# Experts of a perceiver block on one core: up products with the weights stationary and the row columns moving

## The chip, the cores and the metric

The kernel runs on one core of one Trainium2 chip, as a single program: a cross attention, a self attention and a feed-forward part with a shared expert and eight routed ones. The metric is the device time of one execution in microseconds. TensorE multiplies: it loads a stationary operand of up to 128 x 128 (LDWEIGHTS, "PEld" in the profile) and streams a moving operand through it (MATMUL, "PE"), with the result in PSUM. ScalarE (ACT), VectorE (DVE) and GpSimd (POOL) do the elementwise work.

## The reference

Only the last part of the reference matters here. `x` is (8, 128, 512), so 1024 tokens of width 512; the hidden width is 1024.

```python
def _L0_ffn_ref(x, Wg, Wu, Wd, W1, W2):
    xt = x.reshape(T, D)
    probs = jax.nn.softmax(xt @ Wg, axis=-1)
    topv, topi = jax.lax.top_k(probs, 2)
    topv = topv / jnp.sum(topv, axis=-1, keepdims=True)
    cw = jnp.zeros((T, E), x.dtype).at[jnp.arange(T)[:, None], topi].set(topv)
    h = _gelu(jnp.einsum('td,edf->tef', xt, Wu))
    y = jnp.einsum('tef,efd->ted', h, Wd)
    moe = jnp.einsum('ted,te->td', y, cw)
    shared = _gelu(xt @ W1) @ W2
    return (shared + moe).reshape(B, S, D)
x = x + _L0_ffn_ref(_layernorm(x), ...)
```

## The kernel before

The experts' part is the function `experts`. Tokens are handled as tiles of 128 rows: 8 tiles (`NT`) for the shared expert, whose rows are the tokens in order, then the tiles of the eight routed experts, into which each token's normalised row was scattered twice (`rows_scratch`). How many tiles an expert has is known only on the chip; it is read from `first_i` as the bounds of a loop, and with these inputs 29 tiles run in all, 21 of them routed.

A float32 product is made from three float32r products. Every operand is split into a rounded part (`_h`, `hu`, `hd`) and a remainder (`_l`, `lu`, `ld`), and the product is high x high + remainder x high + high x remainder, accumulated in PSUM. In the names, u is an up weight of 512 x 1024 (four chunks of 128 rows, `DC`) and d a down weight of 1024 x 512 (eight chunks, `FC`).

One tile runs as follows, on four engines tied by semaphores:

- ScalarE loads the tile's rows (`load_row`, line 1332), two tiles ahead. TensorE transposes them four times into `rowT_ps` (`turn`, line 1259), ScalarE rounds them to `rowT_h` (line 1336), and VectorE takes the remainder `rowT_l` (line 1393).
- TensorE's up products (lines 1279, 1283, 1289): the stationary operand is a chunk of the transposed rows, the moving one 512 columns of a weight, and `up_ps` has tokens on partitions. Two halves of 512 hidden features, 24 matmuls. The ones with the weight's remainder `lu` come last.
- ScalarE applies gelu to each half (`g`, line 1350). TensorE transposes each half with four transposes (`turn_hidden`, line 1267) into `gT_ps`, so that features are on partitions; between the halves stands `turn` for the next tile. ScalarE rounds to `gT_h` (line 1353), VectorE takes the remainder `gT_l` (line 1399).
- TensorE's down products (lines 1301, 1305, 1309): a 128 x 128 block of `gT` is stationary, 512 columns of a down weight move; 24 matmuls into `down_ps`.
- VectorE adds the result to `x2` (shared expert, line 1406) or scales it to `y` (routed, line 1491), and GpSimd adds `y` to the output with an indirect DMA (`add_rows`, line 1210).

The weights of a later expert are brought in meanwhile, in eight chunks of 512 KB: SyncE loads them (line 1159) when the previous expert's remainders are made, ScalarE rounds them between two experts' tiles (`round_weights`, line 1344), and GpSimd makes the remainders (line 1203). For the shared expert VectorE makes the remainders itself, ahead of its first tile's other work (line 1422). Each engine runs its instructions in the order written; a wait holds back everything behind it on that engine.

Of the kernel before, what the change touches and what calls it, by code (L numbers as in the profile page):

```python
# [12 lines left out]
P = 128  # L13
# [1040 lines left out]
def experts(nc, up_ap, down_ap, out_ap, rows_dram, meta_dram, x2, xn3, logits, raw_u, raw_d, hu0, hd0, raw_in, hi_done, one):  # L1054
# [6 lines left out]
    with ExitStack() as ctx:  # L1061
# [3 lines left out]
        def sem(name):  # L1065
            return ctx.enter_context(nc.semaphore(name))
# [45 lines left out]
        up_ps = ctx.enter_context(nc.psum_tensor("up_ps", [P, NH, 512], F32))  # L1112
        gT_ps = ctx.enter_context(nc.psum_tensor("gT_ps", [P, NH, 4, P], F32))
        down_ps = ctx.enter_context(nc.psum_tensor("down_ps", [P, D], F32))
# [17 lines left out]
        gelu_done = sem("gelu_done")  # L1132
        gT_done = sem("gT_done")
        gTh_done = sem("gTh_done")
# [117 lines left out]
        def _(pe):  # L1252
# [8 lines left out]

            def turn_hidden(t, n):

                pe.wait_ge(gelu_done, t * 2 + (n + 1))
                pe.wait_ge(gTl_done, t * 2 + (n + 2 * AHEAD - 1))
                for i in range(4):
                    mm = nc.tensor.transpose(gT_ps[:, n, i, :], g[:, n, i * P:(i + 1) * P], ident[:, :])  # L1267
                mm.then_inc(gT_done, 1)

            def tile(t, par, chunks):  # L1270

                wu, wd, ru, rd = hu[par], hd[par], lu[par], ld[par]
                pe.wait_ge(hi_done, chunks + DC)
                for n in range(NH):
                    cols = slice(n * 512, (n + 1) * 512)
                    if n == 0:
                        pe.wait_ge(rowTh_done, t + (AHEAD + 1))
                    for c in range(DC):
                        nc.tensor.matmul(up_ps[:, n, :], rowT_h[:, c, :], wu[:, c, cols], start=(c == 0), stop=False)  # L1279
                    if n == 0:  # L1280
                        pe.wait_ge(rowTl_done, t + (AHEAD + 1))
                    for c in range(DC):
                        nc.tensor.matmul(up_ps[:, n, :], rowT_l[:, c, :], wu[:, c, cols], start=False, stop=False)  # L1283
                for n in range(NH):
                    cols = slice(n * 512, (n + 1) * 512)
                    for c in range(DC):
                        if n == 0:
                            pe.wait_ge(lo_done, chunks + (c + 1))
                        mm = nc.tensor.matmul(up_ps[:, n, :], rowT_h[:, c, :], ru[:, c, cols], start=False,  # L1289
                                              stop=(c == DC - 1))  # L1290
                    mm.then_inc(up_done, 1)
                turn_hidden(t, 0)
                turn(t + 1)
                turn_hidden(t, 1)

                pe.wait_ge(hi_done, chunks + CH)
                pe.wait_ge(y_copied, t + AHEAD)
                for f in range(FC):
                    if f % 4 == 0:
                        pe.wait_ge(gTh_done, t * 2 + (f // 4 + 1))  # L1300
                    nc.tensor.matmul(down_ps[:, :], gT_h[:, f, :], wd[:, f, :], start=(f == 0), stop=False)  # L1301
                for f in range(FC):
                    if f % 4 == 0:
                        pe.wait_ge(gTl_done, t * 2 + (f // 4 + 2 * AHEAD + 1))
                    nc.tensor.matmul(down_ps[:, :], gT_l[:, f, :], wd[:, f, :], start=False, stop=False)  # L1305
                for f in range(FC):
                    if f % 2 == 0:
                        pe.wait_ge(lo_done, chunks + (DC + f // 2 + 1))
                    mm = nc.tensor.matmul(down_ps[:, :], gT_h[:, f, :], rd[:, f, :], start=False, stop=(f == FC - 1))  # L1309
                mm.then_inc(down_done, 1)  # L1310
# [19 lines left out]
        def _(act):  # L1330
# [16 lines left out]
            def tile(t, before_load=None):  # L1347
                for n in range(NH):
                    act.wait_ge(up_done, t * 2 + (n + 1))
                    nc.scalar.activation(g[:, n, :], up_ps[:, n, :], ACT.Gelu).then_inc(gelu_done, 1)  # L1350
                for n in range(NH):
                    act.wait_ge(gT_done, t * 2 + (n + 1))
                    nc.scalar.activation(gT_h[:, 4 * n:4 * n + 4, :], gT_ps[:, n], ACT.Copy).then_inc(gTh_done, 1)
                round_row(t + 1)
                if before_load:
                    before_load()
                load_row(t + 2)
# [24 lines left out]
        def _(dve):  # L1382
# [13 lines left out]
            def hidden_rest(t):  # L1396
                for n in range(NH):
                    dve.wait_ge(gTh_done, t * 2 + (n + 1))
                    nc.vector.tensor_tensor(gT_l[:, 4 * n:4 * n + 4, :], gT_ps[:, n], gT_h[:, 4 * n:4 * n + 4, :],
                                            ALU.subtract).then_inc(gTl_done, 1)  # L1400

# [9 lines left out]
            dve.sem_inc(rowTl_done, AHEAD)  # L1411
            dve.sem_inc(gTl_done, 2 * AHEAD)
            dve.sem_inc(y_copied, AHEAD)
# [136 lines left out]
```

## Time and profile before

| | us |
|---|---|
| median of 3 runs | 1783.55 |
| lowest and highest | 1782.42, 1787.43 |
| the profiled execution, its own time | 1783.23 |
| its span | 1781.3 |
| TensorE busy | 1659.7 |
| TensorE weight loads busy | 1305.1 |
| ScalarE, VectorE, GpSimd busy | 649.6, 645.7, 554.2 |

The span is the time that the profiler's records cover, from the first instruction to the last; about 2 us of the execution lie around it. Busy times of different engines overlap. A matmul's record holds its latency, so the distance between two starts in a chain is shorter than one record; where n equal instructions of a chain are reported as one row of the timeline, the distance is the row's time less one record's length, divided by n - 1. The experts' part begins at about 1398 us and ends with the kernel.

### The profile page before, as it was taken

How to read it: one execution, taken by the hardware profiler on the slowest of the kernel's cores; microseconds unless marked ns; L12 is line 12 of the kernel's file. 1: busy time of each engine (PE TensorE's matmuls, PEld its weight loads, DVE VectorE, ACT ScalarE, POOL GpSimd, SP SyncE). 2: the span in 40 equal slices, each digit the busy share in tenths (PEclk: the TensorE clock that was granted, in tenths of full speed). 3: DMA queues.
4: the chain of work that ended last, by engine and by line, in shares of the span. 5: the costliest groups of instructions: out<-in, count | busy, mean ns of one | idle time of the engine just before them, and what ended most of it. 6: DMA issues, size and time to landing. Idle time of an engine off the chain costs nothing. (4 is left out here: it accounts for less than half of the span.)

```text
span 1781.3 us, 24531 instructions
## 1 busy us (share of the span) xinstructions
PE 1659.7 (93%) x9230; PEld 1305.1 (73%) x9231; DVE 645.7 (36%) x1075; ACT 649.6 (36%) x1184; POOL 554.2 (31%) x334
## 2 busy tenths in 40 slices
PE   3899999999999999999999999959777799999998
PEld 2587887888887888888788788734334688887876
DVE  5224433433423523523623622622435432222221
ACT  0134434433433433533533533513332234345431
POOL 4333033033033023123113111013111064768661
PEclk9999999999999999999999999979897799999999
DMA  7511111011011011011011010071000435556521
GB/s 257 196 48 48 30 47 46 26 40 47 26 47 42 26 47 47 24 53 47 24 53 47 24 53 0 0 256 70 0 1 0 166 136 137 170 155 206 146 75 33
DMA packets 72798, 128.98 MB, mean 72 GB/s; under 512 B 12161, under 2 KB 28609, under 8 KB 72769
## 3 DMA queue, kind: packets, MB, share of 16 engines
q1 hardware_dynamic: 40176, 92.14, 15.7%
q10 hardware_dynamic: 27776, 28.06, 5.0%
q0 software_dynamic: 4816, 8.41, 2.5%
q8 instruction: 16, 0.26, 0.1%
q14 instruction: 14, 0.11, 0.0%
HBM read 103.10 MB, written 26.79 MB: 73 GB/s over the span
## 5 line engine op out<-in xcount | busy, mean ns | idle before, releaser
L203 POOL TENSOR_TENSOR ctx_h<-stage,one 128x1024 fp32r<-128x1024 f32 x64 | 121.3, 1895 | 769.5 <-PE ps_t L254 753.9
L254 PE MATMUL ps_s<-ctx_h,wk 128*128 128x512 f32 x1024 | 321.3, 390 | 1.7 <-DVE kT L434 1.7
L254 PE MATMUL ps_t<-wv,ctx_h 128*128 128x512 f32 x1024 | 316.6, 390 | 3.5 <-ACT vt L391 3.5
L452 DVE TENSOR_TENSOR kT<-ps_s,kT 64x512 fp32r<-64x512 f32 x128 | 87.5, 684 | 448.2 <-ACT kT L386 447.4
L254 PEld LDWEIGHTS ps_t<-wv,ctx_h 128*128 128x128 f32 x1024 | 193.0, 189 | 44.0 <-ACT vt L391 3.9
L254 PEld LDWEIGHTS ps_s<-ctx_h,wk 128*128 128x128 f32 x1024 | 192.2, 188 | 42.4 <-issue 2.5
L460 DVE TENSOR_REDUCE smax<-ps_s 128x1 f32<-128x1024 f32 x128 | 150.6, 1218 | 145.8 <-PE ps_s L267 144.8
L254 PE MATMUL ps_t<-wv,ctx_l 128*128 128x512 f32 x512 | 199.9, 390 | 0.0
L254 PE MATMUL ps_s<-ctx_l,wk 128*128 128x512 f32 x512 | 199.2, 389 | 0.0
L377 ACT ACTIVATE probs<-ps_s,nmax 128x1024 f32<-128x1024 f32 x128 | 142.1, 1124 | 91.5 <-DVE nmax L463 91.5
L385 ACT ACTIVATE kT<-ps_s 64x512 fp32r<-64x512 f32 x128 | 75.9, 593 | 265.0 <-PE ps_s L254 248.8
L391 ACT ACTIVATE vt<-ps_t 128x512 f32<-128x512 f32 x128 | 76.4, 598 | 239.3 <-PE ps_t L254 239.3
L206 POOL TENSOR_TENSOR ctx_l<-stage,ctx_h 128x1024 fp32r<-128x1024 f32 x64 | 152.8, 2388 | 5.0
L309 PE MATMUL ps_t<-ident,probs 128*128 128x128 f32 x1024 | 131.8, 277 | 9.1 <-DVE pT L469 8.6
L309 PEld LDWEIGHTS ps_t<-ident,probs 128*128 128x128 f32 x1024 | 111.8, 140 | 28.7 <-DVE pT L469 10.5
L323 PE MATMUL ps_o<-pT,vt 128*64 128x128 f32 x2048 | 124.2, 275 | 0.0
L323 PEld LDWEIGHTS ps_o<-pT,vt 128*64 128x64 f32 x2048 | 110.6, 137 | 14.1 <-issue 14.1
L254 PEld LDWEIGHTS ps_t<-wv,ctx_l 128*128 128x128 f32 x512 | 96.4, 188 | 20.1
L254 PEld LDWEIGHTS ps_s<-ctx_l,wk 128*128 128x128 f32 x512 | 96.1, 188 | 19.6
L266 PE MATMUL ps_s<-kT,qa 128*128 128x512 f32 x256 | 108.5, 424 | 0.0
L1350 ACT ACTIVATE g<-up_ps 128x512 f32<-128x512 f32 x58 | 34.4, 599 | 202.8 <-PE up_ps L1289 202.8
L267 PE MATMUL ps_s<-kT,qb 128*128 128x512 f32 x256 | 100.7, 394 | 0.0
(195 smaller groups left out, 2247.8 us busy)
## 6 DMA issues: line engine op xcount, KB each, us to landing
stage<-in_ctx_dram SPq DMA_DIRECT2D x64, 512.0 KB, 3.7
raw_u<-in_up_dram SPq DMA_DIRECT2D x36, 512.0 KB, 4.2
raw_d<-in_down_dram SPq DMA_DIRECT2D x36, 512.0 KB, 4.1
row<-rows_scratch ACTq DMA_DIRECT2D x31, 256.0 KB, 3.1
rows_scratch<-zero SPq DMA_DIRECT2D x25, 256.0 KB, 3.4
q_scratch<-kT ACTq DMA_DIRECT2D x4, 1024.0 KB, 6.7
qa<-q_scratch ACTq DMA_DIRECT2D x32, 128.0 KB, 3.0
qb<-q_scratch ACTq DMA_DIRECT2D x32, 128.0 KB, 2.9
```

The source lines that it names most:

```text
L203: nc.gpsimd.tensor_tensor(hi, stage[:, slot], one[:, 0:1].unsqueeze(2).broadcast_to([P, 2, QT]), ALU.mult).then_inc(hi_done, 1)
L206: nc.gpsimd.tensor_tensor(lo, stage[:, slot], hi, ALU.subtract).then_inc(split_done, 1)
L254: mm = nc.tensor.matmul(out, w(c), m(c), start=(c + k == 0), stop=(c == DC - 1 and k == 2))
L266: nc.tensor.matmul(ps_s[:, j, :], qa[:, h, :], keys, start=True, stop=False)
L267: mm = nc.tensor.matmul(ps_s[:, j, :], qb[:, h, :], keys, start=False, stop=True)
L309: mm = nc.tensor.transpose(ps_t[:, n % 3, i, :], probs[:, e, (4 * j + i) * P:(4 * j + i + 1) * P], ident[:, :])
L323: mm = nc.tensor.matmul(ps_o[e * XD:(e + 1) * XD, p, :], vt[:, t, h * XD:(h + 1) * XD], pT[:, e, t, :], start=(t == 0), stop=(t == MT - 1))
L377: nc.scalar.activation(probs[:, h % 2, j * 1024:(j + 1) * 1024], ps_s[:, 2 * j:2 * j + 2, :], ACT.Exp, bias=nmax[:, h:h + 1], scale=X_SCAL ...
L385: nc.scalar.activation(kT[0:XD, 0, p, keys], ps_s[0:XD, p, :], ACT.Copy)
L391: nc.scalar.activation(vt[:, 4 * g + t, :], ps_v[:, t % 2, :], ACT.Copy).then_inc(v_copied, 1)
L452: nc.vector.tensor_tensor(kT[XD:P, 0, p, keys], ps_s[0:XD, p, :], kT[0:XD, 0, p, keys], ALU.subtract)
L460: nc.vector.tensor_reduce(smax[:, h, j:j + 1], ps_s[:, 2 * j:2 * j + 2, :] .rearrange("p a n -> p (a n)"), AX_X, ALU.max).then_inc(max_don ...
```

## The change

The operands of the up products are exchanged. The stationary operand is now a block of 128 hidden features of a weight chunk, the moving one the 128 columns (tokens) of a chunk of the transposed rows. The result in `up_ps` has features on partitions and tokens along the free dimension, in eight blocks, four to a bank. All three products of a block (high, row remainder, weight remainder) follow one another, block by block. Gelu of a half thus is already laid out as the down products want it: `turn_hidden` and `gT_ps` are gone, ScalarE rounds `g` itself to `gT_h` right after each gelu, and VectorE takes the remainder from `g`. The down products go half by half: rounded gelu with rounded weight, with the weight's remainder, and the gelu's remainder last. Loads, rounding of weights, routing and write-out are unchanged.

```diff
-            def turn_hidden(t, n):
-
-                pe.wait_ge(gelu_done, t * 2 + (n + 1))
-                pe.wait_ge(gTl_done, t * 2 + (n + 2 * AHEAD - 1))
-                for i in range(4):
-                    mm = nc.tensor.transpose(gT_ps[:, n, i, :], g[:, n, i * P:(i + 1) * P], ident[:, :])
-                mm.then_inc(gT_done, 1)
-
             def tile(t, par, chunks):
 
                 wu, wd, ru, rd = hu[par], hd[par], lu[par], ld[par]
                 pe.wait_ge(hi_done, chunks + DC)
-                for n in range(NH):
-                    cols = slice(n * 512, (n + 1) * 512)
-                    if n == 0:
+                for f in range(FC):
+                    out = up_ps[:, f // 4, (f % 4) * P:(f % 4 + 1) * P]
+                    cols = slice(f * P, (f + 1) * P)
+                    if f == 0:
                         pe.wait_ge(rowTh_done, t + (AHEAD + 1))
                     for c in range(DC):
-                        nc.tensor.matmul(up_ps[:, n, :], rowT_h[:, c, :], wu[:, c, cols], start=(c == 0), stop=False)
-                    if n == 0:
+                        nc.tensor.matmul(out, wu[:, c, cols], rowT_h[:, c, :], start=(c == 0), stop=False)
+                    if f == 0:
                         pe.wait_ge(rowTl_done, t + (AHEAD + 1))
                     for c in range(DC):
-                        nc.tensor.matmul(up_ps[:, n, :], rowT_l[:, c, :], wu[:, c, cols], start=False, stop=False)
-                for n in range(NH):
-                    cols = slice(n * 512, (n + 1) * 512)
+                        nc.tensor.matmul(out, wu[:, c, cols], rowT_l[:, c, :], start=False, stop=False)
                     for c in range(DC):
-                        if n == 0:
+                        if f == 0:
                             pe.wait_ge(lo_done, chunks + (c + 1))
-                        mm = nc.tensor.matmul(up_ps[:, n, :], rowT_h[:, c, :], ru[:, c, cols], start=False,
-                                              stop=(c == DC - 1))
-                    mm.then_inc(up_done, 1)
-                turn_hidden(t, 0)
+                        mm = nc.tensor.matmul(out, ru[:, c, cols], rowT_h[:, c, :], start=False, stop=(c == DC - 1))
+                    if f % 4 == 3:
+                        mm.then_inc(up_done, 1)
                 turn(t + 1)
-                turn_hidden(t, 1)
 
                 pe.wait_ge(hi_done, chunks + CH)
                 pe.wait_ge(y_copied, t + AHEAD)
-                for f in range(FC):
...
+                for n in range(NH):
+                    parts = range(4 * n, 4 * n + 4)
+                    pe.wait_ge(gTh_done, t * 2 + (n + 1))
+                    for f in parts:
+                        nc.tensor.matmul(down_ps[:, :], gT_h[:, f, :], wd[:, f, :], start=(f == 0), stop=False)
+                    for f in parts:
+                        if f % 2 == 0:
+                            pe.wait_ge(lo_done, chunks + (DC + f // 2 + 1))
+                        nc.tensor.matmul(down_ps[:, :], gT_h[:, f, :], rd[:, f, :], start=False, stop=False)
+                    pe.wait_ge(gTl_done, t * 2 + (n + 1))
+                    for f in parts:
+                        mm = nc.tensor.matmul(down_ps[:, :], gT_l[:, f, :], wd[:, f, :], start=False, stop=(f == FC - 1))
                 mm.then_inc(down_done, 1)
...
                 for n in range(NH):
                     act.wait_ge(up_done, t * 2 + (n + 1))
                     nc.scalar.activation(g[:, n, :], up_ps[:, n, :], ACT.Gelu).then_inc(gelu_done, 1)
-                for n in range(NH):
-                    act.wait_ge(gT_done, t * 2 + (n + 1))
-                    nc.scalar.activation(gT_h[:, 4 * n:4 * n + 4, :], gT_ps[:, n], ACT.Copy).then_inc(gTh_done, 1)
+                    act.wait_ge(gelu_done, t * 2 + (n + 1))
+                    nc.scalar.activation(gT_h[:, 4 * n:4 * n + 4, :], g[:, n, :].rearrange("p (f t) -> p f t", f=4),
+                                         ACT.Copy).then_inc(gTh_done, 1)
...
-                    nc.vector.tensor_tensor(gT_l[:, 4 * n:4 * n + 4, :], gT_ps[:, n], gT_h[:, 4 * n:4 * n + 4, :],
-                                            ALU.subtract).then_inc(gTl_done, 1)
+                    nc.vector.tensor_tensor(gT_l[:, 4 * n:4 * n + 4, :], g[:, n, :].rearrange("p (f t) -> p f t", f=4),
+                                            gT_h[:, 4 * n:4 * n + 4, :], ALU.subtract).then_inc(gTl_done, 1)
```

TensorE, the first tile, before. In a row stand the line, the result, the moving and then the stationary operand, the result's shape and how many follow one another:

```order
L1279 MATMUL up_ps<-hu,rowT_h 128x512 x4
L1283 MATMUL up_ps<-hu,rowT_l 128x512 x4
L1279 MATMUL up_ps<-hu,rowT_h 128x512 x4
L1283 MATMUL up_ps<-hu,rowT_l 128x512 x4
L1289 MATMUL up_ps<-lu,rowT_h 128x512 x8
L1267 MATMUL gT_ps<-ident,g 128x128 x4
L1259 MATMUL rowT_ps<-ident,row 128x128 x4
L1267 MATMUL gT_ps<-ident,g 128x128 x4
L1301 MATMUL down_ps<-hd,gT_h 128x512 x8
L1305 MATMUL down_ps<-hd,gT_l 128x512 x8
L1309 MATMUL down_ps<-ld,gT_h 128x512 x8
```

TensorE, the first tile, after: its last feature block of the up products, the row transposes and the down products. Seven more feature blocks, of the same three rows each, stand ahead of these rows.

```order
L1270 MATMUL up_ps<-rowT_h,hu 128x128 x4
L1274 MATMUL up_ps<-rowT_l,hu 128x128 x4
L1278 MATMUL up_ps<-rowT_h,lu 128x128 x4
L1257 MATMUL rowT_ps<-ident,row 128x128 x4
L1289 MATMUL down_ps<-hd,gT_h 128x512 x4
L1293 MATMUL down_ps<-ld,gT_h 128x512 x4
L1296 MATMUL down_ps<-hd,gT_l 128x512 x4
L1289 MATMUL down_ps<-hd,gT_h 128x512 x4
L1293 MATMUL down_ps<-ld,gT_h 128x512 x4
L1296 MATMUL down_ps<-hd,gT_l 128x512 x4
```

The eight transposes into `gT_ps` are gone, the 24 up matmuls of 512 columns have become 96 of 128, and the down products of the first half, with all three factors, come before the second half's.

ScalarE, a tile of a routed expert, before:

```order
L1350 ACTIVATE g<-up_ps 128x512 [waits up_done]
L1349 REGISTER_ALU
L1350 ACTIVATE g<-up_ps 128x512 [waits up_done]
L1353 ACTIVATE gT_h<-gT_ps 128x512 [waits gT_done] x2
L1335 REGISTER_ALU
L1336 ACTIVATE rowT_h<-rowT_ps 128x512 [waits rowT_done]
L1332 ISA
L1332 DMA row<-rows_scratch 128x512
```

ScalarE, the same tile, after:

```order
L1337 ACTIVATE g<-up_ps 128x512 [waits up_done]
L1339 ACTIVATE gT_h<-g 128x512 [waits gelu_done]
L1336 REGISTER_ALU
L1337 ACTIVATE g<-up_ps 128x512 [waits up_done]
L1339 ACTIVATE gT_h<-g 128x512 [waits gelu_done]
L1322 REGISTER_ALU
L1323 ACTIVATE rowT_h<-rowT_ps 128x512 [waits rowT_done]
L1319 ISA
L1319 DMA row<-rows_scratch 128x512
```

The rounding of the first half has moved ahead of the gelu of the second, and it waits for ScalarE's own gelu instead of TensorE's transposes.

## Rows read from the trace of the kernel before

**Rows 1.** The page: busy time of TensorE, and the granted clock in 40 slices
```profile
PE 1659.7 (93%) x9230; PEld 1305.1 (73%) x9231; DVE 645.7 (36%) x1075; ACT 649.6 (36%) x1184; POOL 554.2 (31%) x334
...
PEclk9999999999999999999999999979897799999999
```

**Rows 2.** Stretch of tiles 2 to 29: length, busy PE, PEld, DVE, ACT, POOL, then granted clock
```profile
1417.20:1773.00 355.80, 352.25 (x1685) 286.19 (x1683) 87.74 (x198) 140.41 (x204) 217.48 (x136) 1.00 0.49 135
```

**Rows 3.** Waits, 1400 to 1781 us: total, times, longest
```profile
ACT g L1350 <- PE up_ps L1289: 202.8, 55, 9.3
...
PE gT_ps L1267 <- ACT g L1350: 3.6, 3, 1.5
```

**Rows 4.** Timeline of one tile: start us, us, engine line, out<-in, count
```profile
1605.94 1.10 PE L1279 MATMUL up_ps<-hu,rowT_h 128*128 128x512 f32 x4
...
1609.68 2.00 PE L1289 MATMUL up_ps<-lu,rowT_h 128*128 128x512 f32 x8
1610.68 1.06 ACT L1344 ACTIVATE hd<-raw_d 128x1024 fp32r<-128x1024 f32 x1 [1.52 <-DMA raw_d<-in_down_dram]
...
1612.67 0.66 PE L1267 MATMUL gT_ps<-ident,g 128*128 128x128 f32 x4 [1.00 <-ACT g L1350]
...
1613.17 0.60 PE L1259 MATMUL rowT_ps<-ident,row 128*128 128x128 f32 x4
...
1614.11 2.09 PE L1301 MATMUL down_ps<-hd,gT_h 128*128 128x512 f32 x8
...
1619.73 1.10 PE L1279 MATMUL up_ps<-hu,rowT_h 128*128 128x512 f32 x4
```

**Rows 5.** Groups of lines, 1417 to 1773 us: count, busy us, mean ns, idle before
```profile
L1289 PE MATMUL up_ps<-lu,rowT_h 128*128 128x512 f32 x224 | 55.8, 391 | 0.0
...
L1279 PEld LDWEIGHTS up_ps<-hu,rowT_h 128*128 128x128 f32 x224 | 42.0, 188 | 9.3
...
L1399 DVE TENSOR_TENSOR gT_l<-gT_ps,gT_h 128x512 fp32r<-128x512 f32 x56 | 38.7, 692 | 155.6 <-ACT gT_h L1353 155.5
...
L1353 ACT ACTIVATE gT_h<-gT_ps 128x512 fp32r<-128x512 f32 x56 | 33.4, 596 | 8.1 <-PE gT_ps L1267 8.1
L1350 ACT ACTIVATE g<-up_ps 128x512 f32<-128x512 f32 x56 | 33.2, 599 | 198.1 <-PE up_ps L1289 198.1
...
L1259 PE MATMUL rowT_ps<-ident,row 128*128 128x128 f32 x112 | 16.8, 273 | 0.0
```

**Rows 6.** Timeline of weight loads ahead of 128 and of 64 moving columns
```profile
209.60 0.97 PEld L344 LDWEIGHTS ps_t<-ident,spread 128*128 128x128 f32 x8 [0.17 <-issue]
...
1248.21 3.65 PEld L700 LDWEIGHTS bank<-wvd,xnT 128*128 128x128 f32 x32 [0.84 <-issue]
```

**Rows 7.** Timeline, value products of the cross attention, 64 stationary columns
```profile
172.04 1.97 PE L323 MATMUL ps_o<-pT,vt 128*64 128x128 f32 x32
```

**Rows 8.** Clock by stretch (column before DMA share), and loads at the low clock
```profile
1385.00:1400.00 15.00, 10.18 (x44) 8.97 (x44) 0.67 (x4) 1.79 (x3) 1.38 (x9) 0.50 0.44 157
172.00:180.00 8.00, 8.00 (x91) 6.51 (x89) 3.74 (x5) 5.17 (x10) 0.00 (x0) 1.00 0.20 68
...
1384.92 1.78 PEld L700 LDWEIGHTS bank<-wg,wqlT 128*128 128x128 f32 x8 [3.72 <-DVE logits L1048]
```

**Rows 9.** Timeline of the first tile and the start of the second
```profile
1404.73 3.49 DVE L1422 TENSOR_TENSOR lu<-raw_u,hu 128x1024 fp32r<-128x1024 f32 x3
...
1417.21 1.10 PE L1279 MATMUL up_ps<-hu,rowT_h 128*128 128x512 f32 x4
```

**Rows 10.** Timeline, two plain float32 instructions; line 700: ns min/median/max
```profile
1204.60 1.02 PE L700 MATMUL bank<-wxo,o_in 128*128 128x512 f32 x2
...
L700 PE MATMUL bank<-wxo,o_in x64: 592/592/1222, 1176.8 to 1219.2; 128*128 128x512 f32 x64
...
L700 PEld LDWEIGHTS bank<-wg,wqlT x64: 190/333/338, 1343.0 to 1397.1; 128*128 128x128 f32 x64
```

**Rows 11.** Timeline of the end
```profile
1779.85 0.18 POOL L1249 TENSOR_TENSOR hold<-hold 128x1 f32<-128x1 f32 x1 [3.14 <-DMA out_dram<-y,target]
```

More of the change, by code:

```diff
@@ L1112, in experts @@
         up_ps = ctx.enter_context(nc.psum_tensor("up_ps", [P, NH, 512], F32))
-        gT_ps = ctx.enter_context(nc.psum_tensor("gT_ps", [P, NH, 4, P], F32))
         down_ps = ctx.enter_context(nc.psum_tensor("down_ps", [P, D], F32))
@@ L1132, in experts @@
         gelu_done = sem("gelu_done")
-        gT_done = sem("gT_done")
         gTh_done = sem("gTh_done")
@@ L1293, in tile @@
                 turn(t + 1)
-                turn_hidden(t, 1)
                 pe.wait_ge(hi_done, chunks + CH)
                 pe.wait_ge(y_copied, t + AHEAD)
-                for f in range(FC):
[L1299 to L1309, printed above, removed]
+                for n in range(NH):
[10 more added lines that the diff above has]
+                        mm = nc.tensor.matmul(down_ps[:, :], gT_l[:, f, :], wd[:, f, :], start=False, stop=(f == FC - 1))
@@ L1411, in _ @@
             dve.sem_inc(rowTl_done, AHEAD)
-            dve.sem_inc(gTl_done, 2 * AHEAD)
             dve.sem_inc(y_copied, AHEAD)
```

## The prediction

> **What bounds the kernel now.** The page first: TensorE is busy for 93% of the span, and its granted clock stands at nine tenths or more through the last nine slices, where the experts run [rows 1]. That share is an average, so the expert stage was read by itself. From 1417.2 to 1773.0 us, in which tiles 2 to 29 of the 29 run, TensorE is busy for 352.25 of 355.80 us at a granted clock of 1.00 (2.4 GHz), while VectorE has 87.74, ScalarE 140.41 and GpSimd 217.48 us of work [rows 2]. The view of waits agrees: in the whole stage the matmuls wait for a gelu result three times, 3.6 us in all, and ScalarE waits 202.8 us for up products [rows 3]. So TensorE's own instruction stream sets the end, and 355.80 / 28 = 12.71 us is a tile's price. After the last matmul only a write-out of the last rows follows, to 1781.3 us, and the change doesn't touch it [rows 11].
>
> The timeline of one tile shows what TensorE's stream consists of [rows 4]: up products from 1605.94, then (here after one of the three waits, 1.00 us) 12 transposes, down products from 1614.11 and the next tile at 1619.73. Eight chained matmuls of 512 columns take 2.00 us, and one record is 0.39 long [rows 4, 5], so one starts every (2.00 - 0.39) / 7 = 0.230 us. Four transposes take 0.60, with records of 0.27: one per 0.109 us.
>
> **The change part by part. Up products.** 24 matmuls of 512 moving columns become 96 of 128 columns, each with its own load of 128 stationary columns. The arithmetic is the same, 12,288 columns; only the loads grow from 24 to 96. Before, a load was hidden behind 512 columns. What remains of a load when only 128 columns cover it is the disputed number. The trace of before has no float32r matmul of 128 columns, so I bound it. From below: line 323 runs 32 plain float32 matmuls of 128 columns with loads of 64 stationary columns in 1.97 us, one per 0.055 [rows 7]. From above: a plain float32 instruction of 512 columns starts 1.02 - 0.59 = 0.43 us after the one before it (0.59 is one record), and a product takes two of them, 0.86 us; a quarter of that, for 128 columns, is 0.215, and the 0.230 of the old matmul lies just above [rows 4, 10]. Nearest are two rows with the full load of 128 columns and few moving ones. Line 344 has 128 moving columns: eight loads in 0.97 us, the last 0.19 long, one per 0.111. Line 700 with 64 moving columns: 32 loads in 3.65 us, one per 0.112 [rows 6]. Halving the moving columns changes nothing, so there the load sets the pace, at 0.111 us. A float32r load is no shorter than those (188 ns recorded, against 0.19 us of line 344) [rows 5, 6]. I take 0.111: 96 x 0.111 = 10.66 us in place of 24 x 0.230 = 5.52.
>
> By the Trainium skill, "TensorE: Matmul & The Clock Gate", section "LDWEIGHTS (loading the stationary operand)", a load takes its columns over 1.2, 107 ns for 128; the trace agrees with 0.111 per pair. The same page's "Back-to-back issue gap" speaks for a cheaper change: it gives a stream of pairs about 81 ns at 128 columns and 131 ns at 512. The trace has 230 at 512 [rows 4], so I don't take it; by 81 ns the up part would be 96 x 0.081 = 7.8 us, and the kernel would end at about 1826 us.
>
> **Transposes and waits.** Eight of 12 transposes go, 8 x 0.109 = 0.87 us a tile. The three waits for gelu go too, 3.6 us in the whole stage: ScalarE was late there because it was still rounding the next expert's weights (hd, until 1611.7) [rows 4]; now the first half's gelu is asked for 5.3 us after the up products begin and needed only after 10.7. What is late next? The second half of gelu. It starts at the end of the up products, and gelu, rounding and remainder take 0.60, 0.60 and 0.69 us [rows 5]. TensorE meanwhile has four row transposes (0.44) and 12 down matmuls (2.8), 3.2 us, before it asks for the rounded half, and 1.8 more before it asks for the remainder. That cover is wide enough; were it gone, the 1.2 us would show in each of 28 tiles, 34 us. The next row's transposes are queued before this wait, so their copies on ScalarE come behind gelu and rounding, 2.3 us after the up products' end, and the next tile begins 6.0 us after it. ScalarE and VectorE have the same count of instructions; they now read the gelu from SBUF instead of PSUM, which costs nothing here, since both wait. Loads of raw weights, GpSimd's remainders and the write-out all get more time per expert. Cost of all these: zero, under a TensorE that is slower.
>
> **Down products.** Still 24 of 512 columns, in another order; 1614.11 to 1619.73 was 5.62 us [rows 4], and stays so.
>
> A tile is then 10.66 + 0.44 + 5.6 = 16.70 us, and 28 tiles cost 28 x (16.70 - 12.71) = +111.7 us.
>
> **First tile.** It is worse, for two reasons. VectorE makes the shared expert's remainders itself, and the fourth up chunk is ready at 1404.73 + 3.49 = 1408.2 [rows 9]. Before, these were needed after 16 matmuls; now after eight pairs of the first feature block, so TensorE stands still for some 4 us and can't pass block 0 before about 1408.5. And the clock is low there: 0.50 (1.2 GHz) from 1385 to 1400 [rows 8]. At that level eight loads take 1.78 us with records of 0.33, one per 0.21 [rows 8, 10]. The other 84 pairs take 9.3 us if the clock rises at once and 17.9 if it doesn't; with transposes and down products the tile ends between 1423.9 and 1434.5, against 1417.2 before [rows 9]. Middle: +12 us.
>
> **Sum.** 111.7 + 12 = +124 us on the profiled execution's 1783.23 us (span 1781.3), and that execution stands 0.3 us under the median of 1783.55: **1907 us**. Own range of this case: 109 ns instead of 111 and an early clock give 1896; a pair of 120 ns gives 28 x 96 x 0.009 = +24 and, with a late clock, 1935.
>
> **Rivals.**
> *Narrow float32r is slow.* Below some width one float32r matmul could take the four passes of plain float32. Price: the old matmul's 0.227 to 0.230 a pair, 28 x 96 x 0.116 = +312 on my sum: about 2220 us. For it: plain float32 pays this four times over [rows 10]. Against: nothing, since the trace holds no such instruction; but a 512-column float32r matmul shows none of it. 9%.
>
> *The clock falls in the up part.* The array streams 128 columns (53 ns at 2.4 GHz) in 111 ns. If the clock drops to its low level there, a pair costs 0.21: +274 us over 28 tiles, +45 more where the first eight down matmuls run cold; for half of each up part 2065 us, for all 2226. For it: the logit stage, pairs with 8 moving columns and gaps, stayed at 0.50 [rows 8]. Against: the stretch of 172 to 180 us, transposes and value products of 128 columns between the scores, keeps 1.00, and so does the page's clock line through the whole cross attention [rows 1, 8]. 6%.
>
> *The load is half hidden.* If a load may begin well before the matmul ahead of it starts, the pair lies between 0.055 and 0.111, say 0.083: -75 us on my sum, 1832 us. The page's 81 ns is this case. Against: lines 344 and 700 would show it. 5%.
>
> *Faster than before.* A float32r load fully hidden behind 128 columns, 0.055 a pair: the up products then cost 5.3 us as before, the transposes and waits are saved, and the sum is 1907 - 28 x 96 x 0.056 = 1756 us. It decides from a pair of 0.111 - 124 / (28 x 96) = 0.065 us downwards. For it only line 323, whose load has half the columns [rows 7]. 4%; and 1% lies within 0.3% of the old time.
>
> That the change does nothing is excluded: the built program has 96 up matmuls a tile.
>
> **How the numbers follow.** My forecast has 75%, the rivals 9, 6, 5 and 4, no change 1. The range takes in my case whole and the half-hidden load, 80%: 1820 to 1935; both slow cases and the fast one lie outside. A measurement of this kernel tells 0.3%, 5 us. Faster by more: 0.04; within: 0.01; slower by more: 0.75 + 0.09 + 0.06 + 0.05 = 0.95.
>
> **What would show it.** In the changed kernel's trace: loads of the up lines one per 0.111 us with matmuls of 128 columns starting at the same distance; tiles 16.7 us apart; weight-load busy time up to nearly all of the up part; no wait of a down product for gT; one wait of some 4 us for VectorE's lu in the first tile; granted clock 1.00 from the second tile on. Wrong would make it: pairs at 0.23 or at 0.06, a clock of 0.5 inside tiles, or waits for the second gelu half.

## The result and the profile after

| | before | changed kernel |
|---|---|---|
| median, us | 1785.49 (4 runs, 1782.42 to 1787.60) | 1943.51 (4 runs, 1941.80 to 1950.47) |
| span of the profiled execution | 1781.3 | 1939.9 |
| TensorE busy; its weight loads busy | 1659.7; 1305.1 | 1795.4; 1472.4 |
| VectorE busy | 645.7 | 745.7 |

The changed kernel takes 1.0894 times as long (95% interval 1.0860 to 1.0927). The direction was forecast; the time is 36.5 us above the forecast of 1907 and 8.5 us above the upper end of the range.

The page of the changed kernel, to be held against [rows 1]. Its third line is a group of instructions with its total and its mean in ns:

```profile
PE 1795.4 (93%) x11086; PEld 1472.4 (76%) x11087; DVE 745.7 (38%) x1075; ACT 654.0 (34%) x1184; POOL 554.7 (29%) x334
...
PEclk9999999999999999999999997988678999999999
...
L1386 DVE TENSOR_TENSOR gT_l<-g,gT_h 128x512 fp32r<-128x512 f32 x58 | 139.8, 2428 | 231.3 <-ACT gT_h L1339 231.3
```

TensorE is busy for the same share of the span, and its clock is high but for slices in the self attention and around the first tiles. But VectorE has gained 100 us, all of it in one group: taking the remainder of gelu, which took 692 ns in [rows 5], now 2428 on average. The waits of the experts' part (total, times, longest) answer to [rows 3]:

```profile
ACT g L1337 <- PE up_ps L1278: 364.6, 58, 24.9
...
PE down_ps L1296 <- DVE gT_l L1386: 23.0, 14, 13.3
...
PE up_ps L1278 <- DVE lu L1408: 2.4, 4, 0.7
```

The three waits for gelu are gone, as forecast. In their place the down products wait 14 times for VectorE's remainder, 23.0 us in all and once for 13.3 us; in the first tile the up products wait for VectorE's weight remainders, four times and 2.4 us in all. Three stretches (columns named in the first line) show where the excess lies, beside [rows 2]: the first tile; the one tile with the long wait; and the 25 after it.

```profile
core 0: us, PE busy (x) PEld busy (x) DVE busy (x) ACT busy (x) POOL busy (x), PEclk, DMA share, GB/s
1404.70:1435.60 30.90, 28.54 (x124) 26.59 (x125) 12.06 (x16) 4.48 (x7) 0.00 (x0) 0.58 0.47 154
1469.50:1500.60 31.10, 17.81 (x126) 16.20 (x125) 18.99 (x4) 2.95 (x5) 28.24 (x18) 0.81 0.26 93
1500.60:1931.30 430.70, 421.00 (x3101) 390.60 (x3099) 153.85 (x120) 128.34 (x181) 181.67 (x111) 1.00 0.34 96
```

The first tile takes 30.9 us, with the clock low through its up products; the fourth takes 31.1, and TensorE is busy for 17.8 of them while GpSimd has 28.2 us of work; the 25 tiles after it take 430.7 / 25 = 17.2 us each, where 16.7 was forecast. One by one they are 16.6 or 16.7 us long in eleven cases and 17.6 to 18.1 in fourteen. Thirteen of the fourteen hold one of the other waits, 9.7 us in all; the fifth tile holds none, but begins at the low clock that the long wait left behind. The end of the up products of an undisturbed tile, which begins at 1534.85:

```profile
1542.39 0.61 PE L1278 MATMUL up_ps<-rowT_h,lu 128*128 128x128 f32 x4
1542.84 0.61 PE L1270 MATMUL up_ps<-rowT_h,hu 128*128 128x128 f32 x4
...
1545.52 0.62 PE L1257 MATMUL rowT_ps<-ident,row 128*128 128x128 f32 x4
1545.90 1.17 PE L1289 MATMUL down_ps<-hd,gT_h 128*128 128x512 f32 x4
```

Four pairs start 0.45 us after the four ahead of them. Over the whole up part, from 1534.85 to the transposes at 1545.52, 96 pairs take 10.67 us, so one pair takes 0.111 us. This answers the disputed number.

### The profile page after: what moved, and what is told of

It is laid out like the page before. It is cut to its first block and busy times, and to the rows that moved or that the text cites. A ratio compares the mean times of both kernels' runs of the same rounds, so it can differ in the third digit from the quotient of the medians.

```text
span 1939.9 us, 28130 instructions
## 1 busy us (share of the span) xinstructions
PE 1795.4 (93%) x11086; PEld 1472.4 (76%) x11087; DVE 745.7 (38%) x1075; ACT 654.0 (34%) x1184; POOL 554.7 (29%) x334
## 5 line engine op out<-in xcount | busy, mean ns | idle before, releaser
L1386 DVE TENSOR_TENSOR gT_l<-g,gT_h 128x512 fp32r<-128x512 f32 x58 | 139.8, 2428 | 231.3 <-ACT gT_h L1339 231.3
L1278 PE MATMUL up_ps<-rowT_h,lu 128*128 128x128 f32 x928 | 146.1, 280 | 2.4 <-DVE lu L1408 2.4
L1274 PE MATMUL up_ps<-rowT_l,hu 128*128 128x128 f32 x928 | 145.3, 280 | 0.0
L1270 PE MATMUL up_ps<-rowT_h,hu 128*128 128x128 f32 x928 | 144.1, 279 | 0.8 <-ACT rowT_h L1323 0.8
L1270 PEld LDWEIGHTS up_ps<-rowT_h,hu 128*128 128x128 f32 x928 | 128.2, 197 | 3.6 <-issue 1.1
L1278 PEld LDWEIGHTS up_ps<-rowT_h,lu 128*128 128x128 f32 x928 | 126.2, 197 | 3.1 <-DVE lu L1408 3.1
```

The lines of the kernel that those rows point to most:

```text
L1270: nc.tensor.matmul(out, wu[:, c, cols], rowT_h[:, c, :], start=(c == 0), stop=False)
L1274: nc.tensor.matmul(out, wu[:, c, cols], rowT_l[:, c, :], start=False, stop=False)
L1278: mm = nc.tensor.matmul(out, ru[:, c, cols], rowT_h[:, c, :], start=False, stop=(c == DC - 1))
L1386: nc.vector.tensor_tensor(gT_l[:, 4 * n:4 * n + 4, :], g[:, n, :].rearrange("p (f t) -> p f t", f=4), gT_h[:, 4 * n:4 * n + 4, :], ALU.sub ...
```

## Experiments

**Where VectorE's time goes.** The timeline of the fourth tile (start, length, both in us, then the instruction): GpSimd starts a series of weight remainders, ScalarE has rounded the second half at 1481.6, and VectorE's remainder ends at 1498.65, half a microsecond after GpSimd's two groups of four are through.

```profile
1479.57 9.35 POOL L1201 TENSOR_TENSOR lu<-raw_u,hu 128x1024 fp32r<-128x1024 f32 x4
...
1480.99 0.63 ACT L1339 ACTIVATE gT_h<-g 128x512 fp32r<-128x512 f32 x1
...
1481.65 17.00 DVE L1386 TENSOR_TENSOR gT_l<-g,gT_h 128x512 fp32r<-128x512 f32 x1 [4.67 <-ACT gT_h L1339]
...
1488.88 9.22 POOL L1201 TENSOR_TENSOR ld<-raw_d,hd 128x1024 fp32r<-128x1024 f32 x4
...
1498.71 2.08 PE L1296 MATMUL down_ps<-hd,gT_l 128*128 128x512 f32 x4 [13.29 <-DVE gT_l L1386]
```

The usual case is the same in small: the remainder of a first half (here reported with the short second one, 7.58 us together) ends at about 1632.9, after GpSimd's series has ended at 1632.4, and the down products wait 0.7 us.

```profile
1622.71 9.72 POOL L1201 TENSOR_TENSOR lu<-raw_u,hu 128x1024 fp32r<-128x1024 f32 x4
...
1625.36 0.63 ACT L1339 ACTIVATE gT_h<-g 128x512 fp32r<-128x512 f32 x1
...
1626.02 7.58 DVE L1386 TENSOR_TENSOR gT_l<-g,gT_h 128x512 fp32r<-128x512 f32 x2 [5.47 <-ACT gT_h L1339]
...
1633.05 1.20 PE L1296 MATMUL down_ps<-hd,gT_l 128*128 128x512 f32 x4 [0.68 <-DVE gT_l L1386]
```

Two readings are possible. Before, VectorE read the transposed gelu from PSUM and the rounded one from SBUF; now it reads both from SBUF. Or something else that runs in these stretches (ScalarE's weight rounding, raw weights landing) is in the way.

Experiment 1 gives VectorE its PSUM operand back. Gelu goes to PSUM for this, so ScalarE also writes it there and rounds it from there; nothing else changes.

```diff
-        g = sb("g", [P, NH, 512])
...
+        g = ctx.enter_context(nc.psum_tensor("g_ps", [P, NH, 512], F32))
```

> Theory, port: in the changed kernel VectorE takes the remainder of gelu from two SBUF operands, and in that form it is held up while GpSimd works through a series of weight remainders (mean 2428 ns instead of 692, once 17.0 us). Here gelu is written to the two PSUM banks that gT_ps left free, so VectorE reads one operand from PSUM and one from SBUF again; nothing else changes. Expected: every remainder takes 0.69 us, the down products' waits for it (23.0 us) are gone, the tiles that took 17.6 take 16.7, the one of 31.1 takes 16.7, the clock stays at 1.00 from the second tile on, and the time falls by about 28 us to 1915. Rival, ScalarE or DMA: the remainders are late because of ScalarE's rounding of weights or raw weights landing; then their mean stays near 2.4 us and the time at 1943.

Measured: 1912.32 us (1911.45 to 1915.87), 1.0715 times before (1.0690 to 1.0741). The row of the remainders (shortest, median and longest in ns) and the stretch of tiles 2 to 29:

```profile
L1386 DVE TENSOR_TENSOR gT_l<-g_ps,gT_h x58: 690/692/694, 1418.4 to 1896.7; 128x512 fp32r<-128x512 f32 x58
...
1434.20:1901.00 466.80, 466.80 (x3476) 438.06 (x3476) 87.65 (x198) 142.08 (x204) 216.75 (x136) 1.00 0.35 101
```

No remainder is longer than 0.694 us, no down product waits, TensorE is busy in every microsecond of 466.8 us, and 28 tiles take 16.7 us each. With the operand in PSUM the hold-up is gone, and this is worth 1943.5 - 1912.3 = 31.2 us between the medians. In the two profiled executions tiles 2 to 29 take 495.7 and 466.8 us, 28.9 us less; of the rest, 1.4 us lie ahead of the experts' first up product (at 1404.67 and at 1403.27), where nothing was changed.

Experiment 2 leaves VectorE's operands in SBUF and takes away GpSimd's reading. In it the products with the routed experts' weight remainders add nothing.

```diff
-                    nc.gpsimd.tensor_tensor(weight_chunk(lu[s % 2], ld[s % 2], i), weight_chunk(raw_u, raw_d, i),
-                                            weight_chunk(hu[s % 2], hd[s % 2], i), ALU.subtract).then_inc(lo_done, 1)
+                    nc.gpsimd.memset(weight_chunk(lu[s % 2], ld[s % 2], i).bitcast(F32), 0.0).then_inc(lo_done, 1)
```

> The changed kernel with GpSimd's weight remainders replaced by a fill with zeros of the same size, so the products with the routed experts' weight remainders add nothing; VectorE still reads two SBUF operands. Theory, port, reads: GpSimd no longer reads SBUF, VectorE's remainder takes 0.69 us each time, and the time is about 1915. If GpSimd's writes hold VectorE up as well, remainders of more than 1 us stay. Rival, ScalarE or DMA: mean 2.4 us and 1943 stay.

Measured: 1913.30 us in one run. The row of the remainders, and the fourth tile's fills with the remainder that falls among them:

```profile
L1385 DVE TENSOR_TENSOR gT_l<-g,gT_h x58: 691/693/694, 1419.6 to 1898.0; 128x512 fp32r<-128x512 f32 x58
...
1479.35 3.65 POOL L1201 MEMSET lu<- 128x1024 f32 x4
...
1481.47 0.69 DVE L1385 TENSOR_TENSOR gT_l<-g,gT_h 128x512 fp32r<-128x512 f32 x1 [4.67 <-ACT gT_h L1338]
```

GpSimd still writes the same tiles, if in half the time, ScalarE still rounds and the raw weights still land. VectorE's two SBUF operands alone do no harm, and neither do ScalarE and the DMA: the hold-up comes with GpSimd's subtractions, which read SBUF, and not with its fills, which only write it.

Experiment 3 puts the suspected cause into the kernel before. ScalarE also copies each transposed half into `g`, and VectorE reads it there; the price is two more instructions a tile on ScalarE and a wait ahead of each gelu:

```diff
                     act.wait_ge(up_done, t * 2 + (n + 1))
+                    act.wait_ge(gTl_done, t * 2 + (n + 1))
...
                     act.wait_ge(gT_done, t * 2 + (n + 1))
+                    nc.scalar.activation(g[:, n, :], gT_ps[:, n].rearrange("p f t -> p (f t)"), ACT.Copy)
...
-                    nc.vector.tensor_tensor(gT_l[:, 4 * n:4 * n + 4, :], gT_ps[:, n], gT_h[:, 4 * n:4 * n + 4, :],
+                    nc.vector.tensor_tensor(gT_l[:, 4 * n:4 * n + 4, :], g[:, n, :].rearrange("p (f t) -> p f t", f=4), gT_h[:, 4 * n:4 * n + 4, :],
```

> The kernel before with the suspected cause alone put in: ScalarE also copies each transposed half from gT_ps to SBUF (over g, which is free by then), and VectorE takes the remainder from that copy. ScalarE gets 2 x 0.6 us a tile more. Theory, port: remainders of 7 us while GpSimd makes weight remainders, and since the old order asks for the remainder some 2 us after it starts, a wait of about 5 us in each tile that meets a series; with 12 to 15 such tiles and one longer stall +60 to +90 us, about 1860. Rival: the long remainders belong to the turned layout; then all take 0.69 us, and only ScalarE's extra copies show, under +20 us.

Measured: 1899.77 us (1898.77 to 1900.90), 1.0641 times before (1.0618 to 1.0664), 40 us more than I had expected.

```profile
L1401 DVE TENSOR_TENSOR gT_l<-g,gT_h x58: 677/692/12611, 1411.7 to 1884.0; 128x512 fp32r<-128x512 f32 x58
...
PE down_ps L1305 <- DVE gT_l L1401: 69.2, 15, 10.5
...
1634.50:1641.30 6.80, 4.97 (x12) 3.91 (x13) 2.98 (x3) 0.00 (x0) 1.22 (x1) 0.50 0.48 164
1641.30:1655.00 13.70, 10.18 (x50) 7.84 (x48) 6.19 (x3) 7.42 (x11) 10.24 (x6) 1.00 0.45 118
```

The direction and the mechanism hold: 15 waits, 69.2 us, in the old layout too. What I had left out is the clock: the last two rows are two successive stretches with their granted clock, and the first of them begins within such a wait, of 4.3 us, which ends at 1636.33. The clock is at 0.50 for 6.8 us there, for 3.4 after some other waits, and most disturbed tiles take about 20 us instead of 13.1. The extra copies cost more as well: undisturbed tiles take 13.1 instead of 12.6 us.

**The first tile.** After VectorE's last chunk the up products run without a gap, and yet at the low clock: four pairs from 1412.38, the same distance as at the end.

```profile
1410.40 0.47 PE L1278 MATMUL up_ps<-rowT_h,lu 128*128 128x128 f32 x1 [0.67 <-DVE lu L1408]
...
1412.38 1.05 PE L1278 MATMUL up_ps<-rowT_h,lu 128*128 128x128 f32 x4
...
1427.74 1.05 PE L1278 MATMUL up_ps<-rowT_h,lu 128*128 128x128 f32 x4
```

From 1412.38 to 1427.74 there are 72 pairs, 0.213 us each, and all seven remaining blocks go by like that. Experiment 4 moves the products with the weight remainder into a second pass over the blocks, which takes the four stops out:

```diff
-                    for c in range(DC):
-                        nc.tensor.matmul(out, wu[:, c, cols], rowT_h[:, c, :], start=(c == 0), stop=False)
+                    for c in range(DC):
+                        nc.tensor.matmul(out, wu[:, c, cols], rowT_h[:, c, :], start=(f % 4 == 0 and c == 0), stop=False)
...
+                for f in range(FC):
+                    out = up_ps[:, f // 4, (f % 4) * P:(f % 4 + 1) * P]
+                    cols = slice(f * P, (f + 1) * P)
                     for c in range(DC):
                         if f == 0:
                             pe.wait_ge(lo_done, chunks + (c + 1))
-                        mm = nc.tensor.matmul(out, ru[:, c, cols], rowT_h[:, c, :], start=False, stop=(c == DC - 1))
+                        mm = nc.tensor.matmul(out, ru[:, c, cols], rowT_h[:, c, :], start=False, stop=(f % 4 == 3 and c == DC - 1))
```

> The changed kernel with the products with the weight remainder in a second pass over the eight feature blocks, so that the first tile needs VectorE's weight remainders only after 64 pairs. It tells apart why the first tile takes 31.0 us, at the low clock throughout its up products. Theory, half-filled stream: continuous pairs of 128 columns start at the low clock and don't raise it; only the waits of 2.4 us go, the first tile takes about 28.5 and the time falls by 2 to 3 us, within the noise. Rival, the stops: it is the four stops in the first block that keep the clock low; without them it rises within the up products, the first tile takes 20 to 23 us, and the time falls by 8 to 11 us.

Measured: 1944.94 us (1940.01 to 1945.43), no change from 1943.51. The first tile takes 28.0 us:

```profile
1407.70:1430.00 22.30, 22.27 (x103) 22.11 (x104) 11.05 (x15) 4.26 (x7) 0.00 (x0) 0.50 0.58 202
1430.00:1435.80 5.80, 5.80 (x24) 4.68 (x23) 1.06 (x2) 0.22 (x1) 0.00 (x0) 0.87 0.14 45
```

TensorE is busy for 22.27 of 22.30 us, and the clock is 0.50 through all of them; it rises in the down products. So the stops are not the reason. (The time stays although the first tile is 3 us shorter: the fourth takes 35.1 us here, since there the remainder of the first half falls among GpSimd's eight, and the down products wait 16.3 us for it.) Experiment 9 asks the other way round: 16 matmuls of 512 columns, whose result is overwritten, ahead of the first tile's up products, on the kernel of experiment 1.

```diff
+                if dense:
+                    pe.wait_ge(rowTh_done, t + (AHEAD + 1))
+                for i in range(dense):
+                    nc.tensor.matmul(down_ps[:, :], rowT_h[:, 0, :], wu[:, 0, 0:512], start=(i == 0), stop=(i == dense - 1))
...
-            tile(0, 0, 0)
+            tile(0, 0, 0, dense=16)
```

> The kernel with gelu in PSUM (1912 us), with 16 extra matmuls of 512 columns ahead of the first tile's up products, whose result is overwritten. Theory, half-filled stream: the first tile is slow because its pairs don't raise the low clock, while they keep a high one; the dense matmuls raise it after 4 to 7 us, the up products then run at 2.4 GHz, and the first tile takes about 23 us instead of 31, the kernel 7 to 9 us less, about 1904. Rival: the first tile waits for something else, or the pairs let the clock fall again; then the extra 16 matmuls add 4 to 7 us.

Measured: 1904.00 us (1903.16 to 1905.73), 8.3 us less than experiment 1.

```profile
1403.59 5.90 PE L1267 MATMUL down_ps<-hu,rowT_h 128*128 128x512 f32 x16 [0.78 <-ACT rowT_h L1327]
1409.33 0.56 PE L1274 MATMUL up_ps<-rowT_h,hu 128*128 128x128 f32 x4
...
1401.00:1409.30 8.30, 6.80 (x20) 5.35 (x21) 5.71 (x10) 2.14 (x3) 0.00 (x0) 0.59 0.40 120
1409.30:1426.00 16.70, 16.70 (x125) 15.64 (x124) 6.49 (x7) 2.85 (x5) 0.00 (x0) 1.00 0.63 229
```

Adding 5.7 us of useless work shortens the kernel: the clock rises in the dense matmuls, the pairs of 128 columns keep it, and the first tile takes 16.7 us after them. (The 5.7 us also cover VectorE's four stops, which by experiment 4 are not what keeps the clock low.) Pairs of 128 columns hold a high clock in every tile of these runs without a long wait, and in no first tile made of them alone did they raise a low one. One tile is different, the fifth of the changed kernel, which follows the long wait:

```profile
1500.60:1502.40 1.80, 1.80 (x11) 1.80 (x9) 0.69 (x1) 0.00 (x0) 1.19 (x3) 0.50 0.01 1
1502.40:1504.00 1.60, 1.60 (x16) 1.60 (x16) 0.00 (x0) 0.00 (x0) 1.29 (x2) 0.99 0.48 165
```

There four down products of 512 columns, from 1498.71, stand ahead of the pairs, and the clock rises 1.8 us into the pairs. So pairs of 128 columns alone didn't raise the clock here; pairs that follow a short dense stretch once did.

**What paces a pair.** Experiment 6 halves the moving columns, on the kernel of experiment 1; half of each tile's rows get no up products.

```diff
-                    out = up_ps[:, f // 4, (f % 4) * P:(f % 4 + 1) * P]
+                    out = up_ps[:, f // 4, (f % 4) * P:(f % 4) * P + 64]
...
-                        nc.tensor.matmul(out, wu[:, c, cols], rowT_h[:, c, :], start=(c == 0), stop=False)
+                        nc.tensor.matmul(out, wu[:, c, cols], rowT_h[:, c, 0:64], start=(c == 0), stop=False)
...
```

> The kernel with gelu in PSUM (1912 us), with 64 moving columns in each of the 96 up pairs, so that half of each tile's rows get no up products. Theory, load: a pair is paced by its load, not by its columns; pairs stay 0.11 us apart, tiles at 16.7 and the time at 1912, as long as the clock stays high. Rival, columns: narrow float32r matmuls cost two cycles a column, so a pair falls to 0.055-0.06, tiles to some 11.5 and the time to about 1765. Open beside them: whether the clock holds when the array streams only a quarter of the time in the up part; if it falls for the up part as a whole, pairs take 0.21, tiles some 28, and the time goes to about 2220.

Measured: 2128.49 us in one run. One tile's up products, and the clock of two stretches in it (the column before the DMA share):

```profile
1700.81 0.61 PE L1275 MATMUL up_ps<-rowT_l,hu 128*128 128x64 f32 x4
1701.26 0.61 PE L1279 MATMUL up_ps<-rowT_h,lu 128*128 128x64 f32 x4
...
1702.26 1.04 PE L1275 MATMUL up_ps<-rowT_l,hu 128*128 128x64 f32 x4
...
1716.77 1.11 PE L1258 MATMUL rowT_ps<-ident,row 128*128 128x128 f32 x4
1717.54 2.05 PE L1290 MATMUL down_ps<-hd,gT_h 128*128 128x512 f32 x4
...
1700.00:1701.70 1.70, 1.70 (x17) 1.70 (x17) 0.44 (x1) 0.00 (x0) 0.54 (x2) 1.00 0.00 0
1701.70:1716.70 15.00, 15.00 (x74) 15.00 (x73) 0.69 (x1) 1.18 (x2) 10.53 (x5) 0.51 0.59 157
```

Up to 1701.7 four pairs of 64 columns take 0.45 us, as those of 128 do, so the columns don't pace the pair up to 128. That its load does, and not some other fixed cost of a pair, no run of float32r shows by itself; line 323, with 64 stationary columns and 0.055 us a pair [rows 7], speaks for the load. Then the clock falls inside the up part, 2.6 us after its start at 1699.11, a pair takes 0.213, and the first down products run cold too. With 64 columns the clock falls in every tile (the first has it low from its start), with 128 in none that had no wait. The rival of my prediction in which the clock falls was thus real, half the columns away; its case of "half of each up part" was priced at 2065, and this run, which is slow for more than half, came out at 2128.

Experiment 7 goes the other way: one load of a rounded weight block serves 256 columns, the row's rounded part and its remainder side by side. The row remainder's products aren't added.

```diff
-                    for c in range(DC):
-                        nc.tensor.matmul(out, wu[:, c, cols], rowT_h[:, c, :], start=(c == 0), stop=False)
...
-                    for c in range(DC):
-                        nc.tensor.matmul(out, wu[:, c, cols], rowT_l[:, c, :], start=False, stop=False)
+                    for c in range(DC):
+                        nc.tensor.matmul(up_ps[:, f].rearrange("p k t -> p (k t)"), wu[:, c, cols], rowT[:, c].rearrange("p k t -> p (k t)"),
+                                         start=(c == 0), stop=False)
```

> The changed kernel with the row's rounded part and its remainder side by side, so one load of a rounded weight block serves one matmul of 256 columns instead of two of 128: 64 loads a tile instead of 96, the columns unchanged. The products of the row's remainder land in a PSUM area of their own and aren't added. Theory, load: 32 wide pairs at 0.12 and 32 narrow ones at 0.11 make 7.4 us instead of 10.7, tiles of 13.4, and the time falls by about 92 us to 1852. Rival, columns: two cycles a column at any width under 512, then the wide pair costs 0.22, and the time stays at 1943. For the clock: the half-filled stream theory lets it rise within the first tile's up products, since the wide pairs stream more densely.

Measured: 1911.33 us in one run, a fall of 32 us and not of 92.

```profile
1806.79 0.63 PE L1270 MATMUL up_ps<-rowT,hu 128*128 128x256 f32 x4
...
1811.34 0.69 PE L1270 MATMUL up_ps<-rowT,hu 128*128 128x256 f32 x4
1811.86 0.56 PE L1275 MATMUL up_ps<-rowT,lu 128*128 128x128 f32 x4
...
1814.10 0.62 PE L1257 MATMUL rowT_ps<-ident,row 128*128 128x128 f32 x4
...
PE down_ps L1293 <- DVE gT_l L1383: 65.9, 14, 10.4
```

The up part is 1814.10 - 1806.79 = 7.31 us, as expected from 64 loads, and undisturbed tiles take 13.3. The expectation on the clock came true as well: in the first tile it rises among the up products, and that tile takes 20.2 us.

```profile
1411.00:1416.30 5.30, 5.14 (x24) 5.14 (x25) 4.65 (x5) 0.00 (x0) 0.00 (x0) 0.50 0.92 300
1416.30:1420.30 4.00, 4.00 (x35) 4.00 (x35) 0.69 (x1) 1.23 (x2) 0.00 (x0) 0.95 1.05 400
```

But with shorter up products VectorE's long remainders have less cover: the down products wait 65.9 us for them, where they waited 23.0, and after such a wait the clock is low: it falls 14 times in this trace from the fifth tile on. Most of what the loads gave back went to the hold-up of experiments 1 to 3. How the loss divides between the waits and the clock was not measured.

**The down products' order.** Experiment 8 makes this part of the change alone, in the kernel before (`tile` with its down products as in the change's diff).

> The kernel before with one part of the change alone: the down products half by half, the gelu's remainder last in each half. My account gives this part no cost: same matmuls, the same count of loads, and all waits have cover. Expected within 0.3% of before. Rival: part of the measured slowdown is the new order of the down products; then it is slower by more than 5 us.

Measured: 1787.50 us (1782.18 to 1789.05), ratio 1.0003 (0.9988 to 1.0018). No cost shows, and one of more than about 3 us is excluded.

No run points to a turned version that beats the kernel before: with gelu in PSUM and a dense start it is at 1904, and its undisturbed tile, 16.7 us, is 4 us above the old one.

## Why the prediction was wrong, point by point

- **What bounds the kernel** was right for the kernel before and for experiment 1, where TensorE's stream has no gap in 466.8 us. In the changed kernel it has 14, 23.0 us of waits for VectorE.
- **The price of a pair**, 0.111 us from lines 344 and 700 [rows 6], was right. It was measured at 0.111, and experiment 6 shows that the moving columns don't set it. The rivals of a slow narrow float32r and of a hidden or half hidden load fall. Twenty-eight tiles in experiment 1 take 466.8 / 28 = 16.7 us, as summed.
- **The first tile** had the right parts and the middle of their range, +12 us; it measured 30.97 - 14.66 = +16.3, nearly the upper end, because the clock didn't rise in its up products at all. I had taken a clock that rises halfway with no row for it. This is 4.3 of the 36.5 us. The page's clock line had been misread here too: its last eight slices, not nine, stand at nine tenths, and the ninth from the end, at seven, is the one with the first tile of before. Of the "one wait of some 4 us" for VectorE four short stops of 2.4 us in all came.
- **The step that failed** is the sentence under "Transposes and waits" that ScalarE and VectorE "now read the gelu from SBUF instead of PSUM, which costs nothing here, since both wait". It priced the instruction by its old 0.69 us and asked only whether VectorE had time. Experiments 1 and 2 show what it missed: with two SBUF operands VectorE's subtraction stands still while GpSimd reads SBUF, for a whole series of GpSimd's instructions. Put at zero, it measured 31.2 of the 36.5 us. GpSimd's 217.48 us of work in this stretch stood in [rows 2]; 79.5 + 78.3 = 157.8 of them are its weight remainders (the two rows below), each of which reads two SBUF operands, so the conflict was there to be asked about. The Trainium skill, "SBUF — State Buffer", section "Who interferes with whom", says that a VectorE instruction with two SBUF inputs contends with a GpSimd instruction that reads SBUF and not with one that only writes it. These runs agree on both halves: 17.0 us at most against GpSimd's subtractions, 0.694 us against its fills.

```profile
L1203 POOL TENSOR_TENSOR ld<-raw_d,hd 128x1024 fp32r<-128x1024 f32 x32 | 79.5, 2889 | 0.0
L1203 POOL TENSOR_TENSOR lu<-raw_u,hu 128x1024 fp32r<-128x1024 f32 x32 | 78.3, 2742 | 17.7 <-issue 17.7
```

- **The second half of gelu** was watched. Thirteen of the 14 waits, 9.7 us in all, came for the first half: its remainder, held up for 7 us, begins some 6 us before the down products ask for it, a cover that I hadn't worked out. The longest, 13.3 us in the fourth tile, came for the second half, which the prediction had named as a sign of being wrong, though not for this reason: the 5 us of cover hold a remainder of 0.69 us, not one of 17.0.
- **The rest**, about 1 us, is within the spread of the runs. The profiled executions alone give the same picture: 1939.9 - 1781.3 = 158.6 us, of which 2.1 lie ahead of the first up product of the experts, 16.3 in the first tile and 139.9 in tiles 2 to 29, where 111.7 was forecast.

The range left these out because it widened only terms of TensorE: pair price and clock. A term for VectorE had no upper bound at all.

## What to carry to other kernels

Exchanging the operands of a matmul changes how many loads there are, and with 128 moving columns a float32r pair cost 0.111 us here, as one with 64 did, where one of 512 cost 0.230: four times the instructions at half the price each. When a step is dropped because the data is already in the right layout, look at where its consumers now read: an elementwise instruction that goes from one PSUM and one SBUF operand to two SBUF operands must be held against what GpSimd reads at that time. And a low clock is a cost of its own kind: ask what has to run for it to rise, not only whether the engine is busy.

## What the runs showed of the hardware that I had not expected

- VectorE's subtraction of two SBUF operands was held up not for one GpSimd instruction but for several in a row: 7.0 us over three instructions of 2.9 us or less, and 17.0 us over eight. GpSimd's own instructions kept their length (2866 ns on average for the down chunks, 2889 before).
- TensorE's granted clock stayed at 0.50 for 20 us of gapless pairs of 128 columns (experiment 4) and stayed at 1.00 for 28 tiles that are mostly made of them (experiment 1). With 64 columns it fell in every tile after the first, which was at 0.50 from its start, though pairs had kept their distance of 0.111 us until it fell (experiment 6).
- Sixteen useless matmuls of 512 columns ahead of the first tile made the kernel 8.3 us faster.
